# One block instead of two for the attention and the feed-forward part of a transformer layer

## The reference

```python
x = res + _attn(q, k, v) @ sa_out_w.T        # q, k, v from adaln(x), rotated
x = res + _attn(q, k, v) @ ca_out_w.T        # q from adaln(x), k, v from context
res = x
xn = _adaln(x, noise_emb, ln3_w, ln3_b)
h = jax.nn.gelu(xn @ ffn_w1.T + ffn_b1, approximate=False)
x = res + (h @ ffn_w2.T + ffn_b2)
```

## Time and profile before

| what | value |
|---|---|
| time, median of 3 runs | 1908.3 us (1906.5 to 1909.3) |
| time of the profiled execution | 1905.5 us |
| its span, first to last instruction | 1903.4 us |
| TensorE busy | 1867.2 us, 98% |
| ACT busy | 1429.7 us, 75% |
| VectorE busy | 1285.6 us, 68% |
| GpSimd busy | 801.9 us, 42% |
| DMA traffic | 311.5 MB |

### The profile page before, as it was taken

How to read it: one execution, slowest core, us unless ns; L and a number is a source line. 1 busy time by engine, 2 the same in 40 slices (tenths; PEclk the granted TensorE clock), 3 DMA queues, 4 the chain that set the end, 5 groups by cost and what they waited for, 6 DMA issues and landing times. The chain is left out here.

```text
span 1903.4 us, 38411 instructions
## 1 busy us (share of the span) xinstructions
PE 1867.2 (98%) x13460; PEld 1631.8 (86%) x13460; DVE 1285.6 (68%) x2241; ACT 1429.7 (75%) x3811; POOL 801.9 (42%) x834
## 2 busy tenths in 40 slices
PE   8899999999999999999999999999999999999999
PEld 7788888888878888988988987688898988989898
DVE  5877666767777776776776776346766667666754
ACT  5788878888888898888888899655656566666654
POOL 3534333433443454454454444104535445353531
PEclk9999999999999999999999999999999999999999
DMA  7777777676687687677677688433131322323131
GB/s 219 206 210 209 216 207 204 188 206 188 186 232 212 196 236 221 192 222 220 190 217 223 193 226 201 130 111 122 56 111 56 112 78 93 97 73 105 46 99 34
DMA packets 307375, 311.46 MB, mean 164 GB/s; under 512 B 22000, under 2 KB 259952, under 8 KB 307184
## 3 DMA queue, kind: packets, MB, share of 16 engines
q1 hardware_dynamic: 306576, 308.67, 56.0%
q10 hardware_dynamic: 608, 0.34, 0.1%
HBM read 212.46 MB, written 92.27 MB: 160 GB/s over the span
## 5 line engine op out<-in xcount | busy, mean ns | idle before, releaser
L769 ACT ACTIVATE ps_s<-ps_s,neg_max 128x256 f32<-128x256 f32 x1024 | 461.6, 454 | 52.0 <-DVE neg_max L884 48.8
L884 DVE TENSOR_REDUCE neg_max<-ps_s 128x2 f32<-128x512 f32 x512 | 349.1, 686 | 202.7 <-PE ps_s L640 202.0
L783 ACT ACTIVATE prob<-ps_s 128x512 f32<-128x512 f32 x512 | 307.8, 602 | 89.2 <-PE ps_s L661 85.0
L965 POOL TENSOR_TENSOR rope_c<-rope_c,rope_s 128x256 f32<-128x256 f32 x128 | 98.5, 769 | 316.1 <-DVE rope_s L859 316.1
L640 PE MATMUL ps_s<-kT,qT 96*128 96x256 f32 x1024 | 218.1, 294 | 9.2 <-ACT ps_s L769 4.9
L769 ACT ACTIVATION_READ_ACCUMULATOR ps_s<-ps_s,neg_max 128x1 f32 x1024 | 217.7, 213 | 0.0
L640 PEld LDWEIGHTS ps_s<-kT,qT 96*128 96x128 f32 x1024 | 168.4, 190 | 56.9 <-ACT ps_s L769 21.9
L661 PE MATMUL ps_s<-qT,kT 112*128 112x256 f32 x1024 | 207.7, 285 | 9.6 <-ACT ps_s L769 8.8
L630 PE MATMUL ps_g<-xx_hi,w_hi 128*128 128x256 f32 x1024 | 208.7, 285 | 1.8 <-issue 1.4
L630 PE MATMUL ps_g<-xx_hi,w_lo 128*128 128x256 f32 x1024 | 206.1, 283 | 0.0
L630 PE MATMUL ps_g<-xx_lo,w_hi 128*128 128x256 f32 x1024 | 205.7, 282 | 0.0
(11 more groups left out here) (157 smaller groups left out, 4714.3 us busy)
## 6 DMA issues: line engine op xcount, KB each, us to landing
kT<-k_turned SPq DMA_DIRECT2D x384, 128.0 KB, 3.3
qT<-q_turned SPq DMA_DIRECT2D x128, 256.0 KB, 4.0
f_raw<-in_w1T SPq DMA_DIRECT2D x124, 256.0 KB, 3.0
k_turned<-rot_hi SPq DMA_DIRECT2D x64, 256.0 KB, 3.2
k_turned<-rot_lo SPq DMA_DIRECT2D x64, 256.0 KB, 2.5
q_turned<-rot_hi SPq DMA_DIRECT2D x64, 256.0 KB, 3.8
q_turned<-rot_lo SPq DMA_DIRECT2D x64, 256.0 KB, 4.2
qT<-q_turned SPq DMA_DIRECT2D x128, 128.0 KB, 4.1
```

What stands on the lines that cost most here:

```text
L769: ins = eng.activation(scores[:, t * L:(t + 1) * L], scores[:, t * L:(t + 1) * L], ACT.Exp, bias=neg_max[G % 2][:, t, j:j + 1], accum_out= ...
L783: eng.activation(prob[:, n % NP, :, :].rearrange("p t l -> p (t l)"), ps_s[:, score_bank(step), :], ACT.Exp).then_inc(exp_done, 1)
L884: eng.tensor_reduce(neg_max[G % 2][:, :, j], ps_s[:, score_bank(step), :].rearrange("p (t l) -> p t l", l=L), AX.X, ALU.max, negate=True). ...
L965: eng.tensor_tensor(rope_c[n % 2][:, 0, :], rope_c[n % 2][:, 0, :], rope_s[:, 0, :], ALU.subtract)
```

## The change

The two blocks become one. Each engine gets one function that calls its attention function and then its feed-forward function, so it passes from the one list to the other on its own. What the stop had guaranteed for memory that is used again is now guaranteed by waits: TensorE waits for `exp_done` and `ffn_split` ahead of the up product of chunk 3, and for `res_added` ahead of the first down product; ACT waits for `ffn_split`, `rope_added` and `early_kept` ahead of the first Gelus. The buffers `h_sb`, `h_hi`, `h_lo` and `raw`, which are written first, move to the front of the feed-forward part's memory, and `ps_h` ahead of `ps_y`. The first four raw row loads become a step of the attention list, `rows_ahead`, behind the last residual load and ahead of the last store, with two waits of their own. Some names are changed with no effect.

```diff
         if i == N - 1:
             put(p + 68, "res_load", i)
+            put(p + 70, "rows_ahead")
...
-            def attention_sync(eng):
+            def attention_sync(eng, first_rows):
...
+                    elif kind == "rows_ahead":
+                        first_rows(eng)
...
-            with nc.Block() as block:
-                block.tensor(attention_tensor)
-                block.scalar(attention_scalar)
-                block.vector(attention_vector)
-                block.gpsimd(attention_gpsimd)
-                block.sync(attention_sync)
...
             WF = 2 * P
-            cw_hi, cw_lo = ([sb(f"cw_{part}{n}", [P, 7 * WF], F32R) for n in range(2)] for part in ("hi", "lo"))
-            s_sb = sb("s_sb", [P, 4, WF])
-            NR = 4
-            raw = [sb(f"f_raw{n}", [P, D]) for n in range(NR)]
...
             NH = 3
             h_sb = [sb(f"h_sb{n}", [P, U]) for n in range(2)]
             h_hi = [sb(f"h_hi{n}", [P, U], F32R) for n in range(NH)]
             h_lo = [sb(f"h_lo{n}", [P, U], F32R) for n in range(NH)]
-
+            NR = 4
+            raw = [sb(f"f_raw{n}", [P, D]) for n in range(NR)]
...
+            cw_hi, cw_lo = ([sb(f"cw_{part}{n}", [P, 7 * WF], F32R) for n in range(2)] for part in ("hi", "lo"))
+            s_sb = sb("s_sb", [P, 4, WF])
...
+            ps_h = stage.enter_context(nc.psum_tensor("ps_h", [P, 4, 512], F32))
             ps_y = stage.enter_context(nc.psum_tensor("ps_y", [P, UT, 512], F32))
-            ps_h = stage.enter_context(nc.psum_tensor("ps_h", [P, 4, 512], F32))
...
                         w_h, w_l = up_row(c)
+                        if c == NE:
+                            eng.wait_ge(exp_done, 16 * N_ITEMS)
+                            eng.wait_ge(ffn_split, EARLY)
...
+                        if a == 0:
+                            eng.wait_ge(res_added, sums[N_ITEMS - 1, 1])
                         eng.wait_ge(h_lo_done, a + 1)
...
                         if a == 0:
                             eng.wait_ge(b1_in, 16)
+                            eng.wait_ge(ffn_split, EARLY)
+                            eng.wait_ge(rope_added, len(ropes))
+                        if a < NE:
+                            eng.wait_ge(early_kept, nth["early", a, 1])
...
+            def first_hidden_rows(eng):
+                eng.wait_ge(x_low_done, nth["x_low", N_ITEMS + 1, 1])
+                eng.wait_ge(rot_lo_done, len(ropes))
+                for n in range(NR):
+                    eng.dma_start(hidden_view(n + EARLY, raw[n][:, :]), hidden_row(n + EARLY)).then_inc(fraw_in[n], 16)
...
-                for n in range(NR):
-                    load_row(n)
                 load_x(1, 0)
...
+            def whole_tensor(eng):
+                attention_tensor(eng)
+                hidden_tensor(eng)
...
+            def whole_sync(eng):
+                attention_sync(eng, first_hidden_rows)
+                hidden_sync(eng)
+
             with nc.Block() as block:
-                block.tensor(hidden_tensor)
...
+                block.tensor(whole_tensor)
...
+                block.sync(whole_sync)
```

More of the change, by code:

```diff
@@ L1100, in block_kernel @@
             WF = 2 * P
+            NH = 3
+            h_sb = [sb(f"h_sb{n}", [P, U]) for n in range(2)]
+            h_hi = [sb(f"h_hi{n}", [P, U], F32R) for n in range(NH)]
+            h_lo = [sb(f"h_lo{n}", [P, U], F32R) for n in range(NH)]
+            NR = 4
+            raw = [sb(f"f_raw{n}", [P, D]) for n in range(NR)]
+            x_stats = sb("f_stats", [P, T, 6])
+            x_mv = sb("f_mv", [P, T, 2])
+            x_rstd_in = sb("f_rstd_in", [P, T])
+            x_rstd = sb("f_rstd", [P, T])
+            half_sb = sb("f_half", [P, T])
             cw_hi, cw_lo = ([sb(f"cw_{part}{n}", [P, 7 * WF], F32R) for n in range(2)] for part in ("hi", "lo"))
             s_sb = sb("s_sb", [P, 4, WF])
-            NR = 4
-            raw = [sb(f"f_raw{n}", [P, D]) for n in range(NR)]
             b2_sb = sb("b2_sb", [P, D])
-            xn, f_more = v_kept
+            x_next, f_more = v_kept
             f_res = [res[:, t, :] if t < T else f_more[:, t - T, :] for t in range(UT)]
[L1108 to L1112, removed]
             xb = [[sb(f"xb{j}{half}", [P, 2, L]) for half in range(2)] for j in range(PER)]
@@ L1257, in downs, with x_turn_count @@
                 return down_done, a + 1 - u
-            def turned(u, j, half):
+            def x_turn_count(u, j, half):
                 return 2 * (PER * (u - 1) + j) + half + 1
@@ L1267, in hidden_tensor @@
                         u, j, half = step[1:]
-                        n = turned(u, j, half)
+                        n = x_turn_count(u, j, half)
                         ahead = n
@@ L1363, in copy_sum @@
                     eng.wait_ge(up_done, ups(p, (1, 4, 5)[n]))
-                    eng.activation(u_sb[n][:, :], ps_h[:, bank(p, 1), 0:L], ACT.Copy).then_inc(u_copied, 1)
+                    eng.activation(u_sb[n][:, :], ps_h[:, up_bank(p, 1), 0:L], ACT.Copy).then_inc(u_copied, 1)
                 def second_chunk(p):
@@ L1440, in hidden_scalar @@
                         eng.wait_ge(up_done, ups(p, 6))
-                        eng.activation(h_sb[0][:, 0:L], ps_h[:, bank(p, 4), 0:L], ACT.Gelu, bias=b1_sb[:, c:c + 1]).then_inc(gelu_done, 1)
+                        eng.activation(h_sb[0][:, 0:L], ps_h[:, up_bank(p, 4), 0:L], ACT.Gelu, bias=b1_sb[:, c:c + 1]).then_inc(gelu_done, 1)
                         eng.wait_ge(gelu_done, gelus(a))
@@ L1552, in hidden_gpsimd @@
                             eng.wait_ge(fx_normed, n)
-                        eng.tensor_tensor(rstd[:, :], rstd_in[:, :], half_sb[:, :], ALU.pow).then_inc(f_rstd_done, 1)
+                        eng.tensor_tensor(x_rstd[:, :], x_rstd_in[:, :], half_sb[:, :], ALU.pow).then_inc(f_rstd_done, 1)
                     elif step[0] == "weights":
@@ L1650, in hidden_sync, with whole_scalar, whole_vector, whole_gpsimd @@
                     eng.wait_ge(f_out[j], 16 * (NU - 1 + T))
-            with nc.Block() as block:
-                block.tensor(hidden_tensor)
[L1654 to L1657, removed]
+            def whole_tensor(eng):
+                attention_tensor(eng)
+                hidden_tensor(eng)
+            def whole_scalar(eng):
+                attention_scalar(eng)
+                hidden_scalar(eng)
+            def whole_vector(eng):
+                attention_vector(eng)
+                hidden_vector(eng)
+            def whole_gpsimd(eng):
+                attention_gpsimd(eng)
+                hidden_gpsimd(eng)
+            def whole_sync(eng):
+                attention_sync(eng, first_hidden_rows)
+                hidden_sync(eng)
+            with nc.Block() as block:
+                block.tensor(whole_tensor)
+                block.scalar(whole_scalar)
+                block.vector(whole_vector)
+                block.gpsimd(whole_gpsimd)
+                block.sync(whole_sync)
 def rope_tables(length, half):
```

24 lines of the change are left out of this document (10 added, 14 removed).

## The result

The changed kernel took 1914.6 us, median of 6 runs (1911.7 to 1916.5), against 1906.3 for the kernel before, median of 6 (1905.3 to 1909.3). The ratio is 1.0039, 95% interval 1.0026 to 1.0051: slower by 0.4%, 7.4 us by the ratio and 8.3 by the medians, where I had forecast a gain of 1.8 us and a time between 1903.5 and 1909.5. The profiled execution took 1915.8 us, its span is 1913.8 us against 1903.4. Of the runs further on, one execution of `cw_at_416` (3040.9 us, granted clock 0.556) and one of the kernel before (2749.8 us, 0.685) are in no ratio.

The account below looks back on a forecast made before the run. TensorE, busy 98% of the span, was taken as the bound, with only idle time to gain. Removing the stop saves 1.8 us, all else zero: span 1903.4 to 1901.6, median 1908.3 to 1906.5, range 1903.5 to 1909.5.

Parts of the forecast that it names:

- The stop: Between the last attention matmul and the first up product: removing TensorE's idle time there saves 1.8 us.
- The new waits: Ahead of chunk 3's up product and the first down product: cost nothing, covers 3.7 and 1.9 us.
- the first Gelus: On ACT behind its table load: ready at 1217.5 instead of 1221.59, new waits past by then, cost nothing.
- h_lo(0): VectorE's subtraction behind the residual sums: done about 1221.6, wanted by the first down product at 1222.7, cover 1.1 us.
- the raw rows: Four loads issued behind the residual load, ending about 1211.5, before the store at 1220.8: worth nothing by itself.
- the third rival: At TensorE's transposes of the next x: a late x stops all, 1906.7 or up to 1909.5 us; chance 0.06.
- the port's price: VectorE's first four splits meeting GpSimd's residual adds on a shared port: 1.0 us lost by each, still in time.
- The moved buffers: Feed-forward buffers at new addresses: taken as zero, bounds 3.8 us either way, the down products' summed waits for h_lo.
- The swap of the PSUM tensors: ps_h placed ahead of ps_y: taken as zero, within the same bounds of 3.8 us either way.
- The first rival: New places or phases also remove the later waits for h_lo: gain 5.6 us, 1902.7; chance 0.10.
- The signs of being wrong: TensorE waiting before first down product or x transposes, attention not ending at 1219.9, h_lo waits changing over 1 us.

Follow-up runs that it names:

- cw_at_416: The kernel before with the cw buffers alone moved to the changed kernel's place within 2048 bytes, 416 instead of 224; ratio 1.0022 of before.
- one_block_pad_exact: The changed kernel with pads of 192, 1664 and 192 bytes restoring the old places of h, cw and xf within 2048 bytes; ratio 0.9991 of before.
- u_moved: The kernel before with 64 unused bytes ahead of u_sb alone, which TensorE never touches; ratio 0.9997 of before.
- h_sb_moved: The kernel before with h_sb alone at another place within 128 bytes, behind h_hi and h_lo; ratio 1.0004 of before.
- h_at_224: The kernel before with h_sb, h_hi and h_lo alone moved to the changed kernel's place within 2048 bytes, 224 instead of 416; ratio 1.0017 of before.

## Why the prediction was wrong

- **The stop, -1.8 us: right.** The gap fell from 1.97 to 0.23 us, 1.74 us; `one_block_pad_exact` against before is 1901.7 to 1903.4 in span, with attention parts that end alike, and 0.9991 (0.9982, 1.0000) in time.
- **The new waits, the first Gelus, h_lo(0), the raw rows: right.** Each came in the order forecast and none made TensorE wait. The residual sums ended at 1222.36 and the first down product started at 1224.2, 1.9 us later, as reckoned; h_lo(0) was there at 1222.97, 1.3 us early, reckoned 1.1. That the loads ahead buy nothing was argued and not tried by itself.
- **x late, the third rival: did not happen.** GpSimd's rstd started at 1235.9 and the scaling ended at 1239.8, for transposes at 1243.7. The two adds began before VectorE's last split had ended and took 2.81 us instead of 2.54; no split took longer than 0.69, so the 1.0 us a split of the port's price was not paid.
- **The moved buffers, taken as zero with bounds of 3.8 us either way: this step failed.** It cost 10.5 us, all of it in the pace of matmuls; less the 1.8 of the stop that is 8.7, and the medians moved by 8.3. Slower than 1912.1 us had been given a chance of 0.04. The bounds were sought in the wrong place, in waits between engines, and the evidence that the place hardly matters was VectorE's subtraction, not a matmul. The right rows stood in the chain already: around 1232 us before, 12 up products took 2.80 us and 12 down products of the same shape 2.75. Two paces of one shape, 1.8% apart, over 682 us of TensorE work, give 12 us as an estimate of what new places could cost or gain.
- **The swap of the PSUM tensors: right at zero.** 681.9 for 681.8 us.
- **The first rival** had a gain from new places as its mechanism, priced from h_lo's waits; new places did act, the other way and by another route. The waits for h_lo did shrink, from 3.8 us to 1.4, and gained nothing: in `one_block_pad_exact`, with the old paces, they are 3.9, so it was the slower TensorE that came later for h_lo.
- **The signs of being wrong.** Two came. The waits for h_lo changed by more than 1 us, as an effect of the new pace. The attention part ended 1.6 us later than 1219.9, which says nothing here, since it varies by 6 us with its code unchanged.

The Trainium skill, SBUF — State Buffer, "Who interferes with whom", gives TensorE two SBUF read ports, for the moving operand and the weight load, which are independent of each other and wait for no engine. `u_moved` and `h_sb_moved` agree: moving buffers that only other engines use left the part at 682.0 us. The runs show in addition that TensorE's own pace depends on where its operands lie, and that moving one group changes the pace of a product that doesn't read it. ACT writes h_hi and VectorE h_lo while TensorE works, and no run moves TensorE's reads without these writes. That the starts in the undisturbed pieces of before keep their step of 117 to 119 ns from the first to the last, whatever the other two write meanwhile, speaks against the writes.

What stays open is the mechanism. Shown is that places within 2048 bytes suffice to make the pace fast or slow, that 128 bytes are too short a period to describe it, that the operands act jointly, and that at the same places a pace can depend on what ran before. Every tried place was at a multiple of 32 bytes; which combination is the best, and by what a step is kept or lost from piece to piece, was not found. Each kernel has one trace.

The version to keep is `one_block_pad_exact`: the change with 2048 unused bytes per partition, 0.9991 (0.9982, 1.0000) of before and, by the two ratios, 0.5% faster than the change as made.

## What to carry to other kernels

When a change moves buffers that TensorE reads, its matmuls can change pace by 1 to 3% with no wait to show for it; in a kernel where TensorE is busy for 98% of the time this outweighs any stall of a few us. Read the pace first: duration of a piece divided by its matmuls, per kind of product, and compare equal shapes with each other; two paces for one shape give an idea of what a move can cost. After such a change compare these paces, and if they have changed, restore the places with unused bytes before judging the rest.

## What was not expected of the hardware

- Back-to-back matmuls, each with its own weight load, ran at another pace by the operands' places in SBUF: the down products of 512 columns at a steady 226.7 ns with the old places and 233.3 with the new, those of 256 columns at 113.3 and 117.8 with the old and at 120.0 with the new, with the same data and instructions and a granted clock of 0.998 in both. Other places gave other paces in between.
- At one and the same place the 256-column matmuls kept one of two steps, 113.3 or 117.8 ns, over several pieces, and changed it at transposes and behind a wait (`h_at_224`).
- Placement effects of two groups don't add: +2.0 and +4.3 us apart, +10.6 together.
- They repeat exactly: the part is 681.8 to 682.0 us in five traces with the old places and 692.3 or 692.4 in four with the new, on several chips, while the end of the attention part varied by 6 us.
